# Placing an expert router's products and arithmetic in the middle of the gated layer instead of ahead of it

## The reference, cut to what matters

```python
shared_out = _swiglu(fx @ w_shared_in) @ w_shared_out
logits = fx @ w_gate + gate_bias            # 8 experts
probs = jax.nn.softmax(logits, axis=-1)
top_val, top_idx = jax.lax.top_k(probs, 2)
wdense = zeros((S, 8)).at[arange(S)[:, None], top_idx].add(top_val)
hid = _swiglu(fx @ w1_shared)
routed_out = sum_e wdense[:, e:e + 1] * (hid @ w2[e])
```

## Time and profile before

| | |
|---|---|
| median of 3 runs | 3485.67 us (3479.36 to 3499.95) |
| time of the profiled execution | 3487.78 us |
| its span, first to last instruction | 3486.0 us |
| mean granted TensorE clock over the span | 0.894 of full speed |
| expert stage, turns 0 to 7 | 1986.8 to 2432.9 us of the span |

### The profile page before, as it was taken

One profiled execution on the slowest core, in us unless ns is written; L12 is line 12 of the kernel. 1 busy time (PEld: TensorE's weight loads), 2 busy tenths in 40 slices (PEclk: granted clock), 3 DMA queues, 4 the chain that ended last, 5 costly groups with the idle time before them and its releaser, 6 DMA issues. The chain is left out here.

```text
span 3486.0 us, 89162 instructions
## 1 busy us (share of the span) xinstructions
PE 2856.4 (82%) x34192; PEld 1704.7 (49%) x34192; DVE 2335.6 (67%) x4207; ACT 1588.2 (46%) x2149; POOL 361.4 (10%) x316
## 2 busy tenths in 40 slices
PE   4869999899999989999997599998777820599954
PEld 3322555456645545665652244444555610377733
DVE  1539888788878878888883255545677768244467
ACT  1320767666666666767777311111555520133311
POOL 0245000000000000000002000000111110111024
PEclk8985999999999999999999799999888755799976
DMA  2233011111011111101100100000011220233201
GB/s 96 85 87 77 4 23 24 24 24 24 8 20 23 24 25 24 23 5 24 24 6 5 45 24 12 24 12 2 20 60 62 70 91 9 76 88 88 78 19 36
DMA packets 129573, 130.19 MB, mean 37 GB/s; under 512 B 75748, under 2 KB 107110, under 8 KB 123878
## 3 DMA queue, kind: packets, MB, share of 16 engines
q1 hardware_dynamic: 123494, 120.92, 14.5%
q10 hardware_dynamic: 4224, 4.19, 0.4%
q0 software_dynamic: 1536, 0.40, 0.0%
HBM read 78.41 MB, written 46.66 MB: 36 GB/s over the span
## 5 line engine op out<-in xcount | busy, mean ns | idle before, releaser
L646 DVE TENSOR_REDUCE attn_pm<-attn_MS 128x1 f32<-128x512 f32 (+3 forms) x2304 | 1339.3, 639 | 256.2 <-PE attn_MS L689 231.1
L630 ACT ACTIVATE attn_PT<-attn_ES 128x1024 f32<-128x1024 f32 (+5 forms) x1152 | 1040.0, 951 | 441.0 <-PE attn_ES L723 436.3
L689 PE MATMUL attn_MS<-attn_KX,attn_QX 96*32 96x512 bf16 (+3 forms) x9216 | 1081.0, 382 | 6.0 <-DVE attn_pm L646 4.3
L723 PE MATMUL attn_ES<-attn_QX,attn_KX 99*32 99x512 bf16 (+3 forms) x9216 | 809.0, 369 | 74.9 <-issue 39.1
L738 PE MATMUL attn_OP<-attn_PT,attn_VH 128*17 128x512 f32 (+2 forms) x4608 | 670.0, 566 | 11.8 <-issue 11.7
L689 PEld LDWEIGHTS attn_MS<-attn_KX,attn_QX 96*32 96x32 bf16 x9216 | 394.8, 97 | 306.7 <-issue 106.9
L723 PEld LDWEIGHTS attn_ES<-attn_QX,attn_KX 99*32 99x32 bf16 x9216 | 356.3, 98 | 267.7 <-issue 68.3
L1097 PE MATMUL l0out_ring<-l0out_w,l0out_sT 128*128 128x512 f32 x512 | 228.1, 599 | 0.0
L738 PEld LDWEIGHTS attn_OP<-attn_PT,attn_VH 128*17 128x17 f32 x4608 | 177.5, 99 | 88.8 <-issue 18.5
L685 PE MATMUL attn_MS<-attn_maskb,identb 128*32 128x128 bf16 x2048 | 184.4, 229 | 36.8 <-DMA attn_QX<-qk_parts 25.3
L1011 DVE SCALAR_TENSOR_TENSOR x_res<-l0out_ring,l0out_w,x_res 128x256 f32 (+1 forms) x256 | 123.9, 484 | 99.4 <-PE l0out_ring L1097 94.3
(11 more groups left out here) (275 smaller groups left out, 3279.7 us busy)
## 6 DMA issues: line engine op xcount, KB each, us to landing
attn_KX<-qk_parts SPq DMA_DIRECT2D x96, 128.0 KB, 6.4
attn_QX<-qk_parts SPq DMA_DIRECT2D x96, 128.0 KB, 7.0
vk_beta<-front_vk SPq DMA_DIRECT2D x8, 1024.0 KB, 3.9
kq_transposed<-front_qkG SPq DMA_DIRECT2D x8, 1024.0 KB, 4.2
delta_VK<-vk_beta SPq DMA_DIRECT2D x32, 256.0 KB, 2.8
delta_QK<-kq_transposed SPq DMA_DIRECT2D x32, 256.0 KB, 2.9
attn_out<-attn_OS SPq DMA_DIRECT2D x128, 34.0 KB
x_res<-in_L_attn_x_dram ACTq DMA_DIRECT2D x8, 512.0 KB, 9.5
```

Source lines behind the costliest of these rows:

```text
L630: nc.scalar.activation(PT[u % NPT][:, 512 - wa:512 + wb], ES[half][:, 512 - wa:512 + wb], ACT.Exp, scale=DH ** -0.5).then_inc(exp_done, 1)
L646: nc.vector.tensor_reduce(pm[r][:, i, c:c + 1], MS[slot][:, 0:w], AX.X, ALU.max).then_inc(max_taken, 1)
L689: last = nc.tensor.matmul(MS[slot][r, 0:w], QX[b][0:ROWS, i * P + 32 * g:i * P + 32 * g + 32], KX[b][0:ROWS, 512 * c:512 * c + w], start=n ...
L723: last = nc.tensor.matmul(ES[half][r, o:o + w], KX[b][0:MAXR, kt * P + 32 * g:kt * P + 32 * g + 32], QX[b][0:MAXR, a:a + w], start=not dia ...
```

## The change

The routing products on TensorE, the Exp on ScalarE and the routing arithmetic on VectorE move from ahead of quarter 0 to between quarter 1 and quarter 2. The event names move in the three `Steps` lists in the same way, so that the counts fit the new order. No wait is added or taken away, no product or instruction of the program text is dropped, and SP's queue and POOL's queue are not touched.

```diff
-    V = Steps("lbias", "lmax", ..., "rank", "w", "s_0", "s_1", "s_2", "s_3",
+    V = Steps("s_0", "s_1", "lbias", "lmax", ..., "rank", "w", "s_2", "s_3",
...
-    A = Steps("exp", "sg_0", "sg_1", "sg_2", "sg_3")
-    M = Steps("lg", "ab_0", "ab_1", "ab_2", "ab_3",
+    A = Steps("sg_0", "sg_1", "exp", "sg_2", "sg_3")
+    M = Steps("ab_0", "ab_1", "lg", "ab_2", "ab_3",
...
@@ ScalarE, network(g)
-                act.wait_ge(vd, V(g, "lsub"))
-                nc.scalar.activation(lx[:], lx[:], ACT.Exp).then_inc(ad, 1)
                 for i in range(4):
+                    if i == 2:
+                        act.wait_ge(vd, V(g, "lsub"))
+                        nc.scalar.activation(lx[:], lx[:], ACT.Exp).then_inc(ad, 1)
                     act.wait_ge(md, M(g, f"ab_{i}"))
@@ VectorE
-                route(g)
                 for i in range(4):
+                    if i == 2:
+                        route(g)
                     gate_hidden(g, i)
@@ TensorE, network(g)
-                pe.wait_ge(vd, V(g - 1, f"acc_{J - 1}_0"))
-                for j in range(J):
-                    (the routing products)
                 for i in range(4):
+                    if i == 2:
+                        pe.wait_ge(vd, V(g - 1, f"acc_{J - 1}_0"))
+                        for j in range(J):
+                            (the routing products)
                     if i < 2:
                         pe.wait_ge(vd, V(g - 1, f"acc_{J - 1}_{NEXP}"))
```

More of the change, by code:

```diff
@@ L834, in layer0_out @@
     FM = Steps("wo", "tp", back=0)
-    V = Steps("lbias", "lmax", "lsub", "esum", "erec", "p", "gt", "eq", "eqm", "cnt", "rank", "w", "s_0", "s_1", "s_2", "s_3",
+    V = Steps("s_0", "s_1", "lbias", "lmax", "lsub", "esum", "erec", "p", "gt", "eq", "eqm", "cnt", "rank", "w", "s_2", "s_3",
               *[f"acc_{j}_{e}" for j in range(J) for e in range(NEXP + 1)])
-    A = Steps("exp", "sg_0", "sg_1", "sg_2", "sg_3")
-    M = Steps("lg", "ab_0", "ab_1", "ab_2", "ab_3",
+    A = Steps("sg_0", "sg_1", "exp", "sg_2", "sg_3")
+    M = Steps("ab_0", "ab_1", "lg", "ab_2", "ab_3",
               *[n for j in range(J) for n in (f"sh_{j}", *[f"ex_{j}_{e}" for e in range(NEXP // 2)])])
@@ L1029, in _ @@
                 experts(g, 3)
-            route(G - 1)
             for i in range(4):
+                if i == 2:
+                    route(G - 1)
                 gate_hidden(G - 1, i)
@@ L1061, in network @@
                 pe.wait_ge(fad, FA(g, "hT"))
-                pe.wait_ge(vd, V(g - 1, f"acc_{J - 1}_0"))
-                for j in range(J):
[L1065 to L1069, removed]
-                for i in range(4):
+                for i in range(4):
+                    if i == 2:
+                        pe.wait_ge(vd, V(g - 1, f"acc_{J - 1}_0"))
+                        for j in range(J):
+                            dst = lgp[:, j * NEXP:(j + 1) * NEXP]
+                            for h in range(EH):
+                                last = nc.tensor.matmul(dst, hT[:, h, j * P:(j + 1) * P], wg[:, h, :],
+                                                        start=(h == 0), stop=(h == 1))
+                        last.then_inc(md, 1)
                     if i < 2:
```

## The result

The changed kernel takes 3500.78 us (median of 20 runs, 3489.31 to 3513.63), the kernel before 3486.25 us (20 runs on the same chip): ratio 1.0045, 95% interval 1.003 to 1.006, some 15 us slower. The forecast was +9.8 us and a median of 3495.5 us, within 3483 to 3508.

What follows compares the result with a forecast made beforehand. TensorE's queue bounds the stage: its work plus holes of 2.7 and 1.5 us. 10.2 + 0 + 0 − 1.3 + 0.9 = +9.8 us, a predicted median of 3495.5 us, range 3483 to 3508.

Steps and rivals of the forecast that it cites:

- Turn start, +1.45 us in seven turns (10.2): Ahead of quarter 0, turns 1 to 7: TensorE, no longer covered by routing products, waits for acc_3_8; +10.2 us.
- Quarter 2, nothing gained: At quarter 2 TensorE has no stall for the routing products to fill; 0 us, at most 0.9 gained.
- Routing and table loads hidden: Quarters 2 and 3 on TensorE (6.87 us) cover VectorE's routing (3.96) and two ScalarE table loads (2.57); no cost.
- Turn 0, −1.3: In turn 0 TensorE's clock rises earlier because wide products begin 3.43 us earlier; −1.3 us, between 0 and −1.7.
- the second of the forecast's two cases: Turn 0: the clock rises as long after the wide products begin as now, 3.4 us earlier; worth −1.7 us.
- Falls before the transposes, +0.9: At the 2.7 us hole: longer turns change how often the clock falls; bounds −5.1 and +6.8 us, middle +0.9.
- the three terms: The sum's nonzero parts: turn start +10.2 us, turn 0's clock −1.3, clock falls at the transposes' hole +0.9.
- The stages after are only shifted: Stages behind the expert stage start when it ends and keep their length; no further cost.
- The bound of 0.5%: Whole kernel: 17.4 us, about what a measurement can tell; chances within 0.85, slower 0.13, faster 0.02.
- The forecast's own upper bound: Whole kernel, top of the forecast's clock bounds: 10.2 + 0.9 + 6.8 = +17.9 us.
- quarter 2's bound of 0.9: At quarter 2: at most 0.11 us between s_0's end and the load, 8 times, 0.9 us.

Runs made afterwards that it cites:

- the run with the shorter wait: Changed kernel, but quarter 0 waits for acc_3_4 and quarter 1 for acc_3_8, against the kernel before: 3487.36 us against 3488.14, ratio 0.9997.
- the two later ones: The changed kernel measured twice more, unchanged, each against the kernel before on the same chip: ratios 1.0057 and 1.0067.

## Why the prediction was right, and where its sum was short

- **Turn start, +1.45 us in seven turns (10.2).** Right. Turns without a fall take 56.9 instead of 55.4 us; the wait named is L1012, 7 times (the idle before the first load was 2.01 us where about 1.7 was forecast); taking it away takes the loss away.
- **Quarter 2, nothing gained.** Right: the routing products start with no wait and the queue's pace stands on both sides.
- **Routing and table loads hidden.** Right to a tenth: the Exp ran at once when its input was ready, 0.4 us after its table had been loaded, and the routing ended 1.57 us ahead of need (1.5 worked out). One quarter later the cover is gone, and 1.28 us come out in seven turns, as the run with the routing between quarters 2 and 3 shows.
- **Turn 0, −1.3.** It was −1.9: 20.5, 21.8, 21.9 and 20.4 us in the four profiles with the old order (mean 21.15), 18.9, 19.2, 18.7, 20.2 and 19.3 in five with the new (mean 19.3). The granted clock in the first 3.4 us of the changed kernel's turn 0 and in the next 3.4:

```profile
1979.90:1983.30 3.40, 3.38 (x4) 1.51 (x5) 0.00 (x0) 0.00 (x0) 0.00 (x0) 0.50 0.02 5
1983.30:1986.70 3.40, 3.40 (x9) 1.52 (x8) 0.00 (x0) 1.29 (x2) 0.00 (x0) 1.00 0.00 0
```

  In the earlier trace rows the second stretch, that behind the routing products, is still at half. It holds wide products, so the reason given for −1.3, that these are the only difference between the stretch without a rise and the one with it, is not what the rows say. Over all profiles the clock rises 6.3 to 9.5 us after the turn's first product in the four with the old order and 3.0 to 6.2 us in the nine with quarter 0 first; counted from quarter 0's first product it is 2.9 to 6.1 and 3.0 to 6.2. That is the second of the forecast's two cases, with some 3 us of scatter in either group. Luck has a part in the size: the run with the routing between quarters 0 and 1 took 20.3 us in turn 0, hardly less than the old order's fastest, 20.4.
- **Falls before the transposes, +0.9.** It was more: 5, 6 and 5 instead of 3 and 4, on average 1.8 more, at 1.4 to 1.7 us each, so +2.6 to +3.1 us. The forecast gave the bounds and could not say the number. With turn 0's −1.9 the three terms give +10.9 to +11.4 us; the stage measured +10.3.
- **The stages after are only shifted.** This sentence failed, and with it the step from the stage to the total. The stage alone gives 457.5 − 447.2 = +10.3 us (three profiles against two), which is the forecast's +9.8. The measured medians are 15 to 20 us apart. Part of the rest is in layer 1, 1051.1 to 1062.5 against 1053.4 and 1056.2. Its code is the same; what differs is where the clock stands when it starts. These are the 4 us behind the last addition, before and changed:

```profile
2432.60:2436.60 4.00, 0.00 (x0) 0.00 (x0) 2.15 (x4) 1.49 (x2) 3.71 (x6) 0.65 0.21 33
```

```profile
2437.03:2441.03 4.00, 0.00 (x0) 0.00 (x0) 2.15 (x5) 1.49 (x2) 3.71 (x6) 0.96 0.21 33
```

  The clock falls some 1.2 us after the stage's end in the one and 3.6 in the other. Over all 13 profiles, layer 1 takes 1043 to 1056 us in the six where this fall comes 1.0 to 2.6 us after the stage's end, and 1061 to 1063 in the seven where it comes 2.8 to 4.1 after. The records of the clock go with the time: layer 1 spends 410 to 451 us at the lower level in the first group and 458 to 465 in the second. The kernels with the old order fell into the first group each time (4 of 4), those with another order in 7 of 9 into the second. So the same code can take some 5 to 10 us more through the clock, and an edit ahead of it seems to make that more frequent; 13 profiles suggest it and do not prove it, and the changed kernel itself falls into both groups. That this is the whole excess is not shown: the run with the shorter wait sits in the slow group and measured 0.9997, and a single profile says little of a median. Nor do the profiles hold the excess: attention, whose code is the same too, took 7.9 us less in the three profiles of the changed kernel than in the two of the kernel before, so with +10.3 in the stage and +3.9 in layer 1 their spans differ by only 6.3 us. Where the 4 to 9 us lie by which the medians differ more than the stage stays open.
- **The bound of 0.5%.** I gave 0.85 to a change within it. The first measurement lies within, at 0.45%; the two later ones above. The forecast's centre was too low by 5 to 10 us, and its range held. Two steps on the way to that range were wrong. The forecast's own upper bound adds 0.9 to 10.2 + 6.8; quarter 2's bound of 0.9 is a gain and belongs to the lower end, so the bounds are +2.5 and +17.0 instead of +3.4 and +17.9. And 0.5% is more than what a measurement can tell: the kernel before against itself gave 1.0009 with an interval of 0.16% to either side.

## What to carry to other kernels

Work that seems to stand in the way at a turn's start may be what covers a wait; before moving it, look for what ends last underneath it, here two additions on VectorE. It gains where the queue has a hole, which the list of waits names: the same products behind quarter 3 took 13.0 us off the stage, though only some 8 off the total. A wait on the last of many readers, where the writer needs only the first ones' banks free, costs nothing as long as it is covered, and all of its length when the cover moves. And ask of each idle stretch whether the clock survives it: here removing the one of 2.7 us was worth its length and the falls behind it.

## What was not expected of the hardware

- None of 123 holes of 1.2 to 1.5 us on TensorE, over all profiles, brought a fall of the clock; of the seven holes of 2.7 us in a span, 3 to 6 did, and 13 of 14 where one of 2.7 and one of 2.8 us stood in each of seven turns. Every fall in the stage stands at the end of such a long hole, from 0.6 us before it to 1.4 us after it.
- A table load can run ahead of the wait for its activation's input or behind it. Exp has one wait, and its load ran ahead of it (2106.34, its input ready only at 2107.97). Silu has two, for the products and for VectorE. The trace records one of them as an instruction of its own ahead of the load and the other with the activation. In the loop the one ahead is the wait for the products (2110.86, the load at 2110.93, behind them). In turn 7, with the same two waits in the program, it is the one for VectorE, and the load ran at once behind Exp:

```profile
2397.13 0.23 ACT L908 ACTIVATE l0out_lx<-l0out_lx 128x32 f32<-128x32 f32 x1 [0.46 <-DVE l0out_lx L976]
2397.38 1.28 ACT L914 ACT_TABLE_LOAD   x1
2400.00 0.60 ACT L914 ACTIVATE l0out_sg<-l0out_ring 128x512 f32<-128x512 f32 x1 [1.34 <-PE l0out_ring L1082]
```

  So which wait stands ahead of the load, and not how many there are, decides whether its 1.28 us are hidden.
- A stage with unchanged code differs by up to 20 us (1043 to 1063 for layer 1 in 13 profiles), and its longest times go with the most time at the lower clock (410 us of it in the shortest, 465 in the longest).
